# A two-layer mixture-of-experts block: routing periods in another order, and six shared-expert parts behind the routed tiles

## The reference

```
x = x + 0.5 * ffn(layernorm(x))
x = x + attention(layernorm(x))          # 16 heads, relu on q and k, no softmax
x = x + 0.5 * ffn(layernorm(x))

def ffn(x):
    scores = softmax(x @ gate_w.T)               # 16 experts in 4 groups
    keep the 2 best groups by scores + gate_b, then the 2 best experts in them
    y = sum over the 2 chosen experts of score * (silu(x@We1+be1) * (x@We3+be3) @ We2 + be2)
    z = silu(x@ws1+bs1) * (x@ws3+bs3) @ ws2 + bs2    # the shared expert, hidden size 256
    return y + z
```

## Time and profile before

| | |
|---|---|
| median of 3 runs | 1270.23 us |
| the profiled execution: time, span | 1268.79 us, 1267.1 us |
| PE, DVE, ACT, POOL busy | 91%, 68%, 60%, 55% of the span |
| mean granted TensorE clock | 0.974 |
| layer 1 routing, 30 to 229 us: PE, DVE, ACT, POOL busy | 179.5, 141.9, 79.5, 133.2 us |
| layer 1 routed tiles, 229 to 455 us: PE busy | 222.2 us |
| between tiles and attention, 455 to 484 us: PE busy, granted clock | 11.1 us, 0.79 |
| attention, 484 to 803 us: PE busy | 300.5 us |
| layer 2 routing, 803 to 969 us: PE busy | 148.9 us |
| layer 2 routed tiles, 969 to 1199 us: PE busy | 228.0 us |
| last sums and output, 1199 to 1267 us: PE busy | 37.6 us |

### The profile page before, as it was taken

One profiled execution on the slowest core, in us unless ns is written; L12 is line 12 of the kernel. 1 busy time (PEld: TensorE's weight loads), 2 busy tenths in 40 slices (PEclk: granted clock), 3 DMA queues, 4 the chain that ended last, 5 costly groups with the idle time before them and its releaser, 6 DMA issues.

```text
span 1267.1 us, 26351 instructions
## 1 busy us (share of the span) xinstructions
PE 1149.6 (91%) x6696; PEld 904.2 (71%) x6696; DVE 862.2 (68%) x2774; ACT 761.6 (60%) x1698; POOL 696.6 (55%) x850
## 2 busy tenths in 40 slices
PE   7998899899999967899999999899899999999981
PEld 4554456799999946777877878455466999999751
DVE  6878675466666655768878787676743766666487
ACT  4454341588888845665756654454214888888498
POOL 3576767388888854000411403357561888887820
PEclk9998999999999997999999999999899999999995
DMA  9922227566555533112320300112276566555399
GB/s 354 306 93 76 99 91 198 159 173 177 168 173 158 160 104 104 34 34 67 110 90 27 111 18 34 39 64 92 82 233 235 167 171 173 170 168 156 93 400 369
DMA packets 93928, 181.53 MB, mean 143 GB/s; under 512 B 17592, under 2 KB 60368, under 8 KB 91990
## 3 DMA queue, kind: packets, MB, share of 16 engines
q1 hardware_dynamic: 66342, 110.44, 28.3%
q0 software_dynamic: 26016, 67.55, 15.3%
q10 hardware_dynamic: 1424, 1.86, 0.5%
HBM read 97.63 MB, written 86.08 MB: 145 GB/s over the span
## 4 chain that ended last, share of the span: by engine, by line
PE 56%; DVE 18%; ACT 9%; POOL 6%; issue 5%; DMA 4%; SPq 1%; DVEq 0%; ACTq 0%; POOLq 0%
PE bank L685 20%; PE bank L695 10%; PE bank L544 5%; PE bank L560 5%; PE bank L676 5%; POOL expert_rows L1668 5%; PE bank L791 3%; PE bank L741 2%; ACT rows L1001 2%; DVE stat L1141 2%; PE bank L717 2%; ACT rows L883 1%; ACT xn L1019 1%; DMA expert_rows<-rows,slots 1%; DMA w<-routed_rows 1%
## 5 line engine op out<-in xcount | busy, mean ns | idle before, releaser
L1731 POOL DMA_INDIRECT routed_rows<-xn,rdest x286 | 282.5, 988 | 115.2 <-DVE xn L1450 45.1
L685 PE MATMUL bank<-rows,att 128*128 128x128 f32 x2288 | 302.4, 275 | 0.2 <-ACT att L990 0.2
L685 PEld LDWEIGHTS bank<-rows,att 128*128 128x128 f32 x2288 | 278.3, 192 | 0.8 <-ACT att L990 0.6
L1668 POOL DMA_INDIRECT expert_rows<-rows,slots x160 | 154.7, 967 | 100.8 <-issue 53.0
L990 ACT COPY att<-w 128x512 f32 x286 | 177.1, 619 | 13.4 <-issue 6.7
L1437 DVE SCALAR_TENSOR_TENSOR rows<-bank,tile_b,att 128x128 f32<-128x128 f32 x286 | 100.3, 351 | 108.0 <-ACT att L995 97.8
L695 PE MATMUL bank<-w,rows 128*128 x572 | 170.8, 381 | 2.1 <-DVE rows L1437 2.0
L989 ACT COPY rows<-bank 128x256 f32<-128x256 f32 x286 | 106.6, 373 | 82.3 <-PE bank L676 79.3
L1450 DVE TENSOR_TENSOR xn<-bank,be 128x256 f32<-128x256 f32 x286 | 121.5, 425 | 35.0 <-issue 13.1
L560 PE MATMUL bank<-ws,be 128*128 128x256 f32 x512 | 124.9, 394 | 8.5 <-DVE be L1341 8.5
L560 PEld LDWEIGHTS bank<-ws,be 128*128 128x128 f32 x512 | 98.4, 197 | 40.0 <-DVE be L1341 18.6
(11 more groups left out here) (209 smaller groups left out, 2036.4 us busy)
## 6 DMA issues: line engine op xcount, KB each, us to landing
rows<-expert_rows SPq DMA_DIRECT2D x286, 129.5 KB
rows<-routed_rows SPq DMA_DIRECT2D x32, 512.0 KB, 4.0
w<-routed_rows SPq DMA_DIRECT2D x10, 1024.0 KB, 12.1
w<-in_w SPq DMA_DIRECT2D x2, 4096.0 KB, 19.4
out<-xres SPq DMA_DIRECT2D x16, 512.0 KB, 10.2
xres<-in_x SPq DMA_DIRECT2D x7, 1024.0 KB, 9.8
rows<-routed_rows SPq DMA_DIRECT2D x6, 1024.0 KB, 8.2
expert_rows<-pad SPq DMA_DIRECT2D x47, 129.5 KB, 5.0
```

The costliest lines, as they stand in the source:

```text
L685: last = nc.tensor.matmul(rh_ps[t % RB][:, n * P:(n + 1) * P], m.rw13[:, t % RB, c * C + n * INTER:c * C + (n + 1) * INTER], m.rT[:, t % R ...
L1668: nc.gpsimd.indirect_dma_start(out=d.xg, out_offset=bass.IndirectOffsetOnAxis(ap=m.slots[:, slots_of(r), k, i:i + 1], axis=0), in_=m.xs[bu ...
L1731: nc.gpsimd.indirect_dma_start(out=d.yt, out_offset=bass.IndirectOffsetOnAxis(ap=m.rdest[:, n:n + 1], axis=0), in_=m.ry[:, n, :], in_offse ...
```

## The change

Two things are moved; the same work is done.

In a routing period that is not a layer's first, ACT now does the exponential ahead of the normalising, and the normalising is split: four tiles before the first copy, four behind it. DVE makes the shifted scores first, then the `nmr` that the normalising needs (`negate_mean(r + 1)`, which was the last step of the period before), then the statistics. The steps that DVE takes ahead of a period's first part are fewer.

Six parts of batch 7 in layer 1 are held until the routed tiles are done, where three were. DVE does their adds between and behind the first combines.

```diff
-HELD = ((44, 46, 48), (35, *range(37, PARTS)))
+HELD = ((41, 43, 44, 45, 46, 48), (35, *range(37, PARTS)))
-UPS, DOWNS = (4 * 7 + 2, 4 * 14), (PAIRS * 7 + 2, PAIRS * 14)
-HELD_UP, HELD_DOWN = ((7, 2), (14, 0)), ((7, 1), (14, 0))
+UPS, DOWNS = (4 * 7, 4 * 14), (PAIRS * 7, PAIRS * 14)
+HELD_UP, HELD_DOWN = ((7, 0), (14, 0)), ((7, 0), (14, 0))
 ...
 # ACT, route
-                    if more:
+                    if b == LEAD[L]:
                         normalise(r + 1)
-                    if b == LEAD[L]:
                         exponentials(r)
 ...
                     shared(L, n)
                     exponentials(r)
+                    if more:
+                        normalise(r + 1, range(PAIRS))
                     shared(L, n + 1)
                     if more:
                         copy_xT(r + 1, 0)
+                        normalise(r + 1, range(PAIRS, NT))
                     shared(L, n + 2)
 ...
 # ACT, behind the tiles
-            for n in HELD[0]:
+            for n in HELD[0][0:3]:
                 shared(0, n)
-
             for h in range(PAIRS):
                 weigh_routed(0, h)
+            for n in HELD[0][3:]:
+                shared(0, n)
 ...
 # DVE, route_work
-                    next(chosen)
-                    yield
+                next(chosen)
+                yield
+                if b > LEAD[L] + 1 and b + 1 < BATCHES:
+                    negate_mean(r + 1)
+                if r == 0:
 ...
-                if ahead:
-                    negate_mean(r + 2)
+                if r == 0:
+                    negate_mean(2)
 ...
 # DVE, route: steps ahead of parts
-                    shared(L, n, work, (3 if b > LEAD[L] + 1 else 0) + (5 if b + 2 < BATCHES else 0) + 1)
+                    ahead = b + 2 < BATCHES
+                    shared(L, n, work, (3 if b > LEAD[L] + 1 else 0) + 1 + ahead)
 ...
-                        shared(L, n + 1 + j, work, 17 // others + 1)
+                        shared(L, n + 1 + j, work, (17 + 4 * ahead) // others + 1)
 ...
 # DVE, behind the tiles
-            for n in HELD[0]:
-                shared(0, n, iter(()), 0)
-
-            for h in range(PAIRS):
+            for u in range(3):
+                gated(BATCHES - 1, u)
+            for h in range(2):
+                combine(0, h)
+                add_shared(BATCHES - 1, h)
+            for h in range(2, PAIRS):
                 combine(0, h)
             aggregate(s.a_stats_ready)
+            gated(BATCHES - 1, 3)
             a_negate_mean(0)
+            for p in range(2, PAIRS):
+                add_shared(BATCHES - 1, p)
```

More of the change, by code:

```diff
@@ L1344, in add_shared @@
             def add_shared(r, p):
-                if r == BATCHES - 1 and p == 2:
+                if r == BATCHES - 1 and p == 0:
                     dve.wait_ge(s.bias_added, 1)
```

## The result

The changed kernel takes 1256.67 us, the median of 4 runs (1256.47 to 1256.90), and the kernel before 1269.76 us in 4 runs (1268.96 to 1270.82): a ratio of 0.9896, with a 95% interval of 0.9879 to 0.9914. The forecast was 1255.8 us. The profiled execution of the changed kernel took 1256.47 us with a span of 1254.7, so it is 12.4 us shorter in its span than the profiled one before (1267.1).

The account below looks back on a forecast made before the run. POOL's row sends, stalled for slots, were taken to bound layer 1's routing. Terms -8.2 + 0 + 0.3 - 6.5 = -14.4 us took 1268.79 to 1254.4, plus 1.4 for the median: 1255.8 us, range 1250.5 to 1262.5.

Parts of the forecast that it names:

- Two signs: DVE's `sm` waits below 1 us in periods 3, 5, 14; PE waits 1 to 1.5 at each period's third transpose.
- Exponential ahead: Routing periods 3, 5, 14: PE's 5.6 us of waits go, 1.2 to 1.5 come at the third transpose.
- Period 1 loses 1.45: Layer 1, period 1 has no stall to remove: period 2 and batch 1's slots come 1.45 us later, bounds 0 to 3.2.
- rival A: Routing ring: PE becomes the bound, 1.5 us more in each period, 1261.5 us; chance 0.16.
- Held parts: Ahead of layer 1's tiles: no gain themselves, but keep PE from being next bound; without them -8.2 us would be nothing.
- Low clock at the tiles: Layer 1's first routed tiles: PE restarts at 1.20 GHz, covered by the wait for be2; 0 us, bound 3.
- Attention's start: Behind layer 1's tiles: held parts fill PE's 16.7 us of standing; +0.3 us, bounds -0.5 and +4.
- Layer 2: Layer 2's routing: period 14 gives -4.2 us and the clock -2.3, the next period nothing; -6.5 in all.
- The rule on table loads: ACT's table switches: the skill page's extra drain would delay the silu 1.4 us in four periods; time near 1261.
- Rival B: Layer 1's first tiles: PE's low clock after standing is not covered, +3 to +4 us, 1259.5 us; chance 0.14.
- rival C: Attention's start: exponential gains nothing and the six held parts become the path, +3.8 us, 1274 us; chance 0.03.
- rival D: Routing: period 1 costs nothing and 1.5 us gaps at the turned scores shrink too, 1251 us; chance 0.10.

Follow-up runs that it names:

- ACT's order alone: The change, but only ACT has the new order and DVE keeps statistics ahead of the shift; 1257.09 us, ratio 0.9908.
- order alone: The change's new order of routing periods in both layers, but three parts of layer 1 held as before; 1256.01 us, ratio 0.990.
- the kernel that kept PE running: The change plus 40 unneeded matmuls while PE waits for layer 1's first routed rows; 1256.21 us, ratio 0.9903.
- the better version: The change, but the first reordered period of each layer (batches 1 and 12) keeps the old order; 1251.66 us, ratio 0.9863.
- the held parts alone: The kernel before with six parts held behind the tiles and the old order of routing periods; 1267.63 us, ratio 0.999.
- DVE's half alone: The change, but only DVE has the new order; ACT normalises all eight tiles ahead of the exponential; 1287.97 us, ratio 1.0148.

## Why the prediction was right, and where not

The time and the sign were right, and the place of the gain too: the two stalls of POOL, the exponential before the normalising, the clock of gates 4, 6 and 15, the third transpose's wait of 1.34 us. That the forecast is only 0.9 us off is in part luck. The sum was -14.4 us from profiled execution to profiled execution, and it measured -12.3 (1268.79 to 1256.47); the 1.4 us added for the median then made up for most of that, since the changed kernel's median is only 0.2 above its profiled execution. Two signs were told too sharply: DVE still waits 1.44 us for the exponential in period 14 (below 1 told), and the new wait at the third transpose is 1.34 in periods 1, 3, 5, 12 and 14, but at most 0.7 in 2, 4 and 13. By its own steps:

- *Exponential ahead: 5.6 us of PE's waits in period 3 go and 1.2 to 1.5 come.* Right: 23.79 became 19.15 us. The forecast of 20.3 counted 0.9 us for a later `sel`, which is not late. ACT's order alone carries this (1257.09 us for it alone, 1287.97 without it). The step gave the earlier shift a share in period 3's gain, and it has none there: with DVE's old order period 3 takes 18.86 us.
- *Period 1 loses 1.45.* Too small: the slots of batch 1, and with them its first send, come 2.73 us later. The step had both waits, PE's at the transpose (it measured 1.34 us) and DVE's for the logits (1.68), and took them as largely side by side; they came nearly in a row, PE waiting 1.30 us for `sel` behind the 1.34. It lay inside the bounds of 0 to 3.2. The 1.28 us too little account for the last send, which is 7.06 us sooner and not 8.2. Period 4 is 0.9 us longer than the step counted (24.68 us for 25.51 - 2.1 + 0.4 = 23.8; rival A has 23.4 for it), by PE's waits of 0.77, 0.19 and 0.66 us at its transposes, but behind a landing that POOL sets (ACT stands 1.27 us for it at 112.64), so POOL loses nothing by that.
- *Held parts: nothing by themselves, but without them the -8.2 would be nothing.* The first half is right; the second failed, by the run with order alone (1256.01 us). The step compared PE's new need with PE's old clock time. PE's periods follow the same ring as POOL's, so PE came forward 6.7 us by itself (gate of period 7 at 171.78 for 178.51).
- *Low clock at the tiles: 0.* Right for layer 1, shown by the kernel that kept PE running. The cover is be2.
- *Attention's start: +0.3.* It measured +0.4: from the tiles' end to the first keys 32.26 us before and 32.65 after. The way was as told: a wait of 7.11 us for the last gated part (7.7 told), 5.97 us for the down part (5.5), then full clock. The step left out that the full clock goes on into the keys, 0.56 us more. With order alone the stretch is 31.85, so against that the three parts cost 0.8.
- *Layer 2: period 14 -4.2, clock -2.3, "the next loses nothing".* Period 14 gave 4.87 and the clock 2.31, but period 12 cost 1.6. That step failed: it took the wait at the ranks as cover for the later statistics, but the wait at the ranks is still there (1.41 us) and the transpose's 1.34 came on top. In all -5.6 for -6.5.
- *The rule on table loads.* The Trainium skill, "ScalarE: Activation LUTs", What ACT_TABLE_LOAD costs, adds a drain of some 1.38 us to the load, which would have made 1261. In the changed kernel too the load at 96.26 takes 1.28 us and the silu starts at 97.55. No drain is seen in these rows.

Rival A (PE as the bound of the ring) had the right kind of loss, some 1.5 us in a period, but it decides only in the first reordered period of each layer, where no stall was there to remove; that is what the better version takes back. Rival B is refuted by the kept-running kernel, rival C by the held parts alone. In rival D, the 1.52 us at the turned scores stayed as they were; but for period 1 at no cost, the time of 1251 us is what the better version reaches (1251.66), by that mechanism and the same one in period 12.

## What to carry to other kernels

Where an in-order engine holds a piece of work that waits for something far away (here a landing) ahead of a short one that everybody waits for, put the short one first; but do it only in the periods that have the stall, since the reordered work adds waits where there was slack. If two engines are reordered together, find out which one must go first: ACT's half of this change has its whole gain (1257.09 us for 1256.67), DVE's half alone is slower than doing nothing, and yet DVE's adds 3.8 us where ACT's stands and the first periods keep the old order (1251.66 for 1255.48). And when one engine's chain is shortened in a ring, recompute the arrival of all the others before calling one of them the next bound.

## What the runs showed of the hardware

Seven microseconds of layer 1's tiles at 1.2 GHz in place of 2.4 moved nothing, since DVE stood for the 1 MB of biases with either (its first add of them at 233.45 and 233.54). At the start of layer 2's tiles, two rows of eight matmuls at the low clock (2.05 and 1.64 us for 1.16 and 1.06) cost 1.6 us. The clock fell there in some executions and not in others. The time from the last send to the load of the tiles varies between 3.42 us (217.14 after 213.72) and 4.76 us (219.64 after 214.88) over the executions of this case. So a stage time of a single profile is to be trusted to about 1 us, and to 1.6 across layer 2's first tiles. PE that stood 7 us restarts at half clock and is at full clock again within the next down part (5.97 us for 3.62), while after 16.11 us of standing two pairs of transposes (1.94 us each) still ran at half.
